# The positive part of the softplus by VectorE from PSUM in all chunks, and beats 47 to 63 set anew

## The reference

```python
x_in, res = jnp.split(x @ W_in, 2, axis=-1)
x_conv = silu(_causal_dw_conv(x_in, conv_w, conv_b))           # u
dt, Bm, Cm = jnp.split(x_conv @ W_x, [DT_RANK, DT_RANK + N_STATE], axis=-1)
delta = jax.nn.softplus(dt @ W_dt + b_dt)
A = -jnp.exp(A_log)
# per step: h = exp(delta * A) * h + delta * B * u;   y = sum over n of h * C
y = _selective_scan(x_conv, delta, A, Bm, Cm, D)
x = _layernorm(x + (y * silu(res)) @ W_out)
x = _layernorm(x + (silu(x @ wg.T) * (x @ wu.T)) @ wd.T)
```

## Time and profile before

| | |
|---|---|
| median of 3 runs | 1870.64 us (1870.13 to 1873.51) |
| span of the profiled execution, first to last instruction | 1865.8 us |
| difference of the two: what lies around the span | 4.8 us |
| TensorE busy | 1715.3 us, 92% |
| VectorE busy | 1705.4 us, 91% |
| GpSimd busy | 1651.8 us, 89% |
| ScalarE busy | 1636.9 us, 88% |
| granted TensorE clock, mean | 0.979 |

### The profile page before, as it was taken

The page is one execution under the profiler, slowest core; times in us unless marked ns, Lnnn a source line. Parts: engine busy times, 40 slices in busy tenths (PEclk is TensorE's granted clock), DMA queues, the critical chain, the costliest instruction groups (busy, mean ns, idle before and its releaser), DMA issues.

```text
span 1865.8 us, 32487 instructions
## 1 busy us (share of the span) xinstructions
PE 1715.3 (92%) x10128; PEld 1287.3 (69%) x10128; DVE 1705.4 (91%) x1958; ACT 1636.9 (88%) x2769; POOL 1651.8 (89%) x1629
## 2 busy tenths in 40 slices
PE   8879898998989999898998989999898998988788
PEld 3546676776767677676776767677676776767667
DVE  5989999999999999999999999999999999999994
ACT  5798988989899898998989899898998989898774
POOL 3989899998989989899898999989899898989970
PEclk9999999999999999999999999999999999999999
DMA  7213123141231314214141231313214041221100
GB/s 240 109 46 136 47 71 134 35 159 47 103 102 58 125 47 142 63 60 145 35 151 55 99 106 58 125 47 135 70 58 147 36 147 57 87 96 41 62 23 24
DMA packets 82107, 164.56 MB, mean 88 GB/s; under 512 B 10369, under 2 KB 28033, under 8 KB 81938
## 3 DMA queue, kind: packets, MB, share of 16 engines
q1 hardware_dynamic: 80498, 160.90, 25.1%
q10 hardware_dynamic: 1440, 1.58, 0.3%
HBM read 87.47 MB, written 8.91 MB: 52 GB/s over the span
## 4 chain that ended last, share of the span: by engine, by line
PE 65%; ACT 22%; POOL 7%; issue 4%; DVE 2%; DMA 0%; DVEq 0%; SPq 0%; ACTq 0%; POOLq 0%
PE fill L524 10%; PE ht_upper L699 9%; PE ht_lower L699 9%; PE y_upper L724 8%; PE fill L639 8%; POOL dbu L1185 6%; PE fill L608 5%; PE fill L629 5%; ACT da L1052 4%; ACT gt L1061 3%; PE fill L539 3%; ACT L1140 2%; ACT L1129 2%; PE fill L578 2%; ACT kb L948 2%
## 5 line engine op out<-in xcount | busy, mean ns | idle before, releaser
L1185 POOL TENSOR_TENSOR dbu<-du,brep 128x512 f32<-128x512 f32 x1024 | 1310.6, 1306 | 152.3 <-DVE h L1360 128.7
L1360 DVE TENSOR_TENSOR_SCAN h<-da,carry,dbu 128x512 f32<-128x512 f32 x960 | 1186.9, 1269 | 92.5 <-ACT da L1052 90.7
L1052 ACT ACTIVATE da<-delta,a_s 128x512 f32<-128x512 f32 x960 | 655.7, 689 | 97.2 <-DVE h L1360 89.8
L1061 ACT ACTIVATE gt<-ht_upper,ct 128x512 f32<-128x512 f32 x512 | 348.5, 681 | 62.7 <-PE ht_upper L699 55.7
L699 PE MATMUL ht_upper<-ident,h 128*128 128x128 f32 x2048 | 317.7, 278 | 67.7 <-DVE h L1360 57.3
L699 PEld LDWEIGHTS ht_upper<-ident,h 128*128 128x128 f32 x2048 | 245.9, 143 | 185.9 <-DVE h L1360 102.8
L1372 DVE SCALAR_TENSOR_TENSOR acc<-ht_lower,ct,acc 128x512 f32<-128x512 f32 x480 | 348.6, 726 | 22.4 <-PE ht_lower L699 22.4
L699 PE MATMUL ht_lower<-ident,h 128*128 128x128 f32 x2048 | 317.0, 278 | 39.4 <-DVE acc L1372 34.9
L724 PE MATMUL y_upper<-ident,gt 128*128 128x128 f32 x2048 | 316.6, 278 | 0.0
L699 PEld LDWEIGHTS ht_lower<-ident,h 128*128 128x128 f32 x2048 | 243.8, 143 | 103.0 <-issue 50.4
L724 PEld LDWEIGHTS y_upper<-ident,gt 128*128 128x128 f32 x2048 | 245.8, 143 | 72.1 <-ACT gt L1061 39.6
(11 more groups left out here) (189 smaller groups left out, 1871.9 us busy)
## 6 DMA issues: line engine op xcount, KB each, us to landing
brep<-b_rows SPq DMA_DIRECT2D x127, 512.0 KB, 3.8
xs<-xin SPq DMA_DIRECT2D x242, 256.0 KB, 2.5
xr<-x SPq DMA_DIRECT2D x16, 512.0 KB, 4.2
xt_s<-x_t SPq DMA_DIRECT2D x15, 512.0 KB, 5.1
out<-xr SPq DMA_DIRECT2D x15, 512.0 KB, 3.9
win_s<-w_in SPq DMA_DIRECT2D x2, 512.0 KB, 5.0
h<-xin SPq DMA_DIRECT2D x4, 256.0 KB, 4.0
h<-xin ACTq DMA_DIRECT2D x4, 256.0 KB, 4.5
```

What stands on the lines that cost most here:

```text
L1052: nc.scalar.activation(dst[:, :], delta[:, par, m, :], ACT.Exp, scale=a_s[:, m, n:n + 1])\
L1061: nc.scalar.activation(gt[:, (n * UPPER + k) % GT, :], ht_upper[:, :], ACT.Copy, scale=ct[:, par, k, n:n + 1])\
L1185: nc.gpsimd.tensor_tensor(dbu[:, beat % DBU, :], du[:, par, m, :], brep[:, n // PIECE % 2, n % PIECE, :], ALU.mult).then_inc(dbu_ready, 1)
L1360: nc.vector.tensor_tensor_scan(h[:, n % 2, m, 0:T], da[beat % 2][:, :] if slot is None else da_ahead[:, slot, :], dbu[:, beat % DBU, :], c ...
```

## The change

The Relu on ScalarE and the addition on GpSimd go. In each chunk VectorE does the positive part of the next chunk's block m, max(bank, 0) + delta, in the beat after the one in which ScalarE reads the bank (`READ_AT` + 1), behind its scan, its sum and its back work of that beat. The bank of `dt{m}` is now given back by that instruction. GpSimd keeps the multiplication by u, at the same beats. Some beats from 47 on are set anew in both tables; `dt0` and `dt1` are read at 48 and 52 instead of 49 and 51, `dt2` still at 55, `dt3` at 60 instead of 59, the ups and downs mostly later.

```diff
-           "up0": (45, 46), "up1": (47, 47), "ct": (47,), "dt0": (47,), "up2": (49, 49), "up3": (49, 49),
-           "dt1": (50,), "up4": (51, 51), "up5": (51, 51), "dt2": (52,), "down0": (53, 54, 54, 54, 54, 55),
+           "up0": (45, 46), "up1": (47, 47), "ct": (47,), "dt0": (47,), "up2": (49, 49), "up3": (50, 50),
+           "dt1": (51,), "up4": (52, 52), "up5": (54, 54), "dt2": (54,), "down0": (55, 55, 56, 56, 57, 57),
...
@@ def times_u
-            d = delta[:, par, m, :]
-
-            eng.wait_ge(relu_ready, (c - 1) * DB + m + 1)
-            eng.wait_ge(softplus_step, (c * DB + m + 1) * 3)
-            unit.tensor_tensor(d, d, du[:, par, m, :], ALU.add).then_inc(delta_ready, 1)
             eng.wait_ge(delta_ready, c * DB + m + 1)
-            unit.tensor_tensor(du[:, par, m, :], d, u[:, par, m, :], ALU.mult).then_inc(du_ready, 1)
+            unit.tensor_tensor(du[:, par, m, :], delta[:, par, m, :], u[:, par, m, :], ALU.mult).then_inc(du_ready, 1)
@@ TensorE: when a bank is free
-                taken[f"dt{m}"] = (softplus_step, 3 * DB, 3 * m + 1)
+                taken[f"dt{m}"] = (delta_ready, DB, m + 1)
@@ ScalarE: read_front
-                        if c:
-                            nc.scalar.activation(du[:, par, m, :], b[:, :], ACT.Relu).then_inc(relu_ready, 1)
                         nc.scalar.activation(d, b[:, :], ACT.Abs).then_inc(softplus_step, 1)
@@ VectorE (first_u calls it too)
+            def positive_part(c, par, m):
+
+                d = delta[:, par, m, :]
+                dve.wait_ge(softplus_step, 3 * (c * DB + m + 1))
+                nc.vector.scalar_tensor_tensor(out=d, in0=front_bank(c, f"dt{m}")[:, :], scalar=0.0, in1=d,
+                                               op0=ALU.max, op1=ALU.add).then_inc(delta_ready, 1)
@@ VectorE: step, behind back()
+                    for m in [] if isinstance(i, int) and i == NCH - 1 else range(DB):
+                        if READ_AT[f"dt{m}"] + 1 == beat:
+                            positive_part(i + 1, 1 - par, m)
```

More of the change, by code:

```diff
@@ L48 @@
 GT = 4
-READ_AT = {"conv0": 14, "conv1": 20, "conv2": 22, "conv3": 26, "ct": 48, "down0": 55, "down1": 57, "down2": 63,
[1 row of a table removed]
+READ_AT = {"conv0": 14, "conv1": 20, "conv2": 22, "conv3": 26, "ct": 48, "down0": 58, "down1": 59, "down2": 62,
[1 row of a table added]
            "gate3": 42, "gate4": 42, "gate5": 44, "o0": 12, "o1": 15, "o2": 18, "o3": 20, "res0": 24, "res1": 25,
[1 row of a table removed]
[1 row of a table added]
            "x1t1": 33, "xin0": 2, "xin1": 4, "xin2": 4, "xin3": 9, "yt0": 8, "yt1": 10}
@@ L226, in mamba_swiglu @@
         xd_ready, ct_ready, softplus_step = sem("xd_ready"), sem("ct_ready"), sem("softplus_step")
-        relu_ready = sem("relu_ready")
         delta_ready, du_ready, b_written = sem("delta_ready"), sem("du_ready"), sem("b_written")
@@ L1427, in first_u @@
             def first_u(m):
-                d = delta[:, 0, m, :]
-                dve.wait_ge(softplus_step, 3 * (m + 1))
-                nc.vector.scalar_tensor_tensor(out=d, in0=front_bank(0, f"dt{m}")[:, :], scalar=0.0, in1=d,
-                                               op0=ALU.max, op1=ALU.add).then_inc(delta_ready, 1)
+                positive_part(0, 0, m)
                 dve.wait_ge(delta_ready, m + 1)
                 dve.wait_ge(conv_raw, FIRST_CONVS.index(m) + 1)
-                nc.vector.tensor_tensor(du[:, 0, m, :], d, u[:, 0, m, :], ALU.mult).then_inc(du_ready, 1)
+                nc.vector.tensor_tensor(du[:, 0, m, :], delta[:, 0, m, :], u[:, 0, m, :], ALU.mult).then_inc(du_ready, 1)
             dve.wait_ge(a_exp, 1)
```

## The result

| | before | after |
|---|---|---|
| median of the runs | 1870.6 us (1870.13 to 1873.51) | 2024.97 us (2021.42 to 2026.71) |
| span of the profiled execution | 1865.8 us | 2022.9 us |
| mean granted TensorE clock | 0.979 | 0.952 |

A forecast was written before the change was run, and what follows sets the result against it. VectorE's own work bounds the stretch, TensorE with as little room. Work 2.44, new idle 3.8 less 0.68, plus 0.6: 6.1 us a chunk, fourteen 85.4, chunk 0 0.7; sum 86 on 1870.6 gives 1957 us, range 1910 to 1972.

The forecast's parts named there:

- Step 1: Scan of beat 49: its factor comes behind block 0's softplus on ScalarE, 1.35 us of new VectorE idle time.
- Step 2: Beats 50 to 53: up3 waits for the positive part, dt1 is late, 0.14 us idle before the scan of 53.
- Step 3: Beats 54 to 56: up5 waits for the positive part, dt2 follows; 0.25 us idle before the sum, 0.84 before scan 56.
- Step 4: Beats 57 to 61: down1 cannot start before 920.76, dt3 starts at 924.6; 0.90 us idle before the scan of 61.
- Step 5: Beats 62 and 63: TensorE holds down3 until the positive part ends; VectorE waits 0.3 us for down3.
- Work: Four positive parts a chunk added to VectorE, 0.61 us each, 2.44 us in all (bounds 1.8 to 2.7).
- GpSimd: 60 additions of 1274 ns removed, 5.1 us a chunk, worth 0.
- rival C: Positive parts need the port VectorE shares with GpSimd, 0.68 us more each, 41 us on top, 1998 us; chance 0.03.
- Rivals A and B: A: only the work stays, 1907 or 1918 to 1928 us, 0.30; B: positive parts fall into waits, 1842 us, 0.05.

The follow-up runs named there:

- both cures: Kernel after with ten more transposes on TensorE ahead of up5 in beat 54, and up5's product ahead of the sum on VectorE at beat 55: 1983.52 us.
- ten transposes: Kernel after with ten more transposes on TensorE in the gap ahead of up5 at beat 54, into the bank ht_lower: 2000.50 us.
- up5's product first: Kernel after with one swap on VectorE: at beat 55 the product of up5 stands ahead of the sum: 2001.09 us.
- tables alone: Kernel before with the new FILL_AT and READ_AT only; Relu on ScalarE, addition on GpSimd, bank given back by the Abs as before: 1969.79 us.
- the code alone: The change's code with the tables of before, the positive part in the beat of the read, ahead of the back work: 1941.58 us.
- the second experiment: Kernel after with the Relu on ScalarE again, the max over it in SBUF, and the dt bank given back by the Abs: 2028.23 us.
- odd beats in the new tables: Kernel before with the new tables, but dt0, dt1 and dt3 read at beats 49, 53 and 61: 1947.14 us.

## Why the prediction was wrong

Times of scans in us from beat 48's, in chunk 7:

| scan of beat | 49 | 53 | 56 | 61 | next chunk's first |
|---|---|---|---|---|---|
| predicted | 2.55 | 10.54 | 18.30 | 27.71 | 34.21 |
| after | 2.53 | 10.64 | 19.89 | 30.96 | 37.66 |
| after, both cures | 2.54 | 10.66 | 18.47 | 28.36 | 35.05 |

The clock's part is seen when the stretches of chunks 1 to 14 are sorted by how often the granted clock falls in them (us, in brackets the number of chunks):

| kernel | no fall | one | two |
|---|---|---|---|
| after | none | 37.7 (5) | 38.8 to 39.2 (9) |
| after, ten transposes | 36.0 (8) | 37.4 to 37.7 (6) | none |
| after, up5's product first | 35.05 (2) | 36.2 to 36.4 (7) | 38.0 (5) |
| after, both cures | 35.05 (10) | 36.4 to 36.7 (3) | 37.6 (1) |

- **Step 1** (beat 49, factor late, 1.35): right. 1.25 us of idle time, the scan 0.02 us from its place.
- **Step 2** (beats 50 to 53): right to 0.1. up3 does wait 1.23 us for the positive part, dt1 is late, the scan of 53 idles 0.20 (forecast 0.14). That holds for chunk 7 and the four like it. In the other nine the clock falls behind up3's gap, and the scan of 53 idles 1.3 to 1.6: the first place at which the missing term shows.
- **Step 3** (beats 54 to 56) failed in size in every chunk, and in chunk 7 it is the first step that failed. The term that was mis-sized is the time of the matmuls behind a gap, for which I had no lower clock. The chain is the one written down, up5 behind the positive part of block 1 and dt2 behind up5, but I gave up5 0.97 us, dt2 1.05 and the turn 0.6, as they run without a gap ahead. Behind one of 1.83 us they took 1.79, 1.91 and 0.83, the sum was late by 1.85 instead of 0.25, and the scan of 56 came 1.6 us behind its forecast. Filling the gap took 24.5 us off the kernel.
- **Step 4** (beats 57 to 61) failed in its chain. I let down0 run as if its bank were free. It shares up5's, and up5's product stands behind the sum that step 3 made late; TensorE waited 1.10 us there, and the scan of 61 was late by another 1.66. My own times show the slip: up5's product would end at about 918.1, six parts, two turns and a back turn later it is about 922.0, and not 920.76, when down1 can start. The row is in the order of VectorE shown ahead of the prediction (`kb<-fill1`, behind the sum). The product ahead of the sum took 24 us off, 14 of them by this wait and the rest by the clock.
- **Step 5** (down3): 0.47 of idle time instead of 0.3; right in kind.
- **Work**: four positive parts of 0.6, right. **GpSimd** 0, right. **The port** (rival C) is out: 665 to 685 ns. Rivals A and B are out: the waits came, and nothing got shorter.
- **Attribution**: I counted the waits as the price of the held bank. The tables alone cost 98 us, the code alone 70, both 154. So the waits of steps 1, 2 and 4 are there in full without a held bank, from the tables (with a Relu more in each softplus), and those of step 3 to less than a third (0.70 us of 2.41). The two causes overlap by about 14 us (98 + 70 - 154; about, since the positive part stands in another beat in the code-only kernel).

**The sum.** The span grew by 157 us where 86 were forecast. Of the 71 between them, the clock makes 35: the stretch takes 38.50 us on average and 36.03 with the clock up, 2.47 in each of fourteen chunks. The bank of down0 makes 14 (36.03 against 35.05). What else my trace forward has too short makes 12 (35.05 against 34.21; in chunk 7 with both cures the surplus is 0.17 us by beat 56, 0.65 by 61 and 0.84 at the end). Chunk 15 with the tail behind it, which I took as 0, costs 6, and chunk 0 cost 2.0 us instead of 0.7. About 4 us are spread over the rest. With both cures 111 us remain in the median.

The Trainium skill (TensorE: Matmul & The Clock Gate, section "Part 1: The HAM clock gate") has the array's clock follow how busy TensorE was just before, with two levels and no other. The traces agree on the levels: they have 0.50 and 1.00 alone, and 0.52 is the mean of a window with both. Which gap brings a fall they don't tell by its length alone, as the last section shows. I gave the clock no term. A trace forward that opens gaps on TensorE needs one: here a second price of some 1.6 us behind a wait of 1.8.

Open: how much of the tables' 98 us falls to each entry other than dt0 (42 by itself in the old tables) and dt3 (4), the held bank's price under the new tables, which the second experiment mixes with four Relus, and what decides whether the clock falls behind a gap.

No kernel here beats the one before. The best form of the change is the code with the old tables, 83 us faster than the kernel after.

## What to carry to other kernels

When a change brings both code and a table of places, price the table as a change of its own, by following what each in-order engine has ahead of the entry that others wait for; and when an instruction moves behind a late one, ask which bank it gives back. Where a trace forward opens an idle stretch on TensorE, work out the matmuls behind it at the lower clock too. Moving a reader by a beat is nearly free where its engine is ahead of the one that waits for it (dt3, 4 us), and dear where that one already waits (dt0, 42 us). One chunk is not all chunks: where the clock falls in some and not in others, sort them by it before you read a price from one.

## What the runs showed of the hardware

TensorE's granted clock fell from 1.00 to 0.50 in stretches in which the engine was otherwise at work, behind gaps of 1.2 to 1.9 us, but not behind each such gap. Of the fourteen chunks with both neighbours' work, it fell in 14 behind the gap of 1.83 us before up5 and in 9 behind that of 1.23 before up3 (kernel after), in 9 behind 1.32 (dt0 read at 48), in 6 behind 1.85 before up3 (the code without the tables), in 2 after 1.83 before dt1 (odd beats in the new tables) and in none behind 1.7 (tables alone). So the length of a gap by itself does not say whether the clock falls. One of the twelve chunks of the odd-beats kernel in which it stays up, with dt1's projection at its usual length:

```profile
939.38 1.10 PE L578 MATMUL fill<-xd,wdt_s 128*128 128x512 f32 x2 [1.83 <-DVE kb L1283]
...
937.50:943.50 6.00, 4.09 (x22) 2.70 (x22) 6.00 (x7) 4.73 (x8) 4.62 (x5) 1.00 0.05 16
```

The same 10128 matmuls were busy for 1715 us at a mean clock of 0.979 and for 1776 at 0.952. A VectorE instruction with both operands in SBUF took up to 1551 ns beside GpSimd's work, with one in PSUM at most 685.
